# A cross-attention and mixture-of-experts kernel: first maximum behind the logits' copy, w2's first third behind w3, w2 and the turned h in two float32r parts

## What is computed

```python
# LayerNorm of x, then cross-attention with 16 heads of 16
Q = split_heads(layernorm(x) @ Wq + bq); K = split_heads(ctx @ Wk + bk); V = split_heads(ctx @ Wv + bv)
scores = einsum('bhqd,bhkd->bhqk', Q, K) / sqrt(16)
x = x + tanh(g_xattn) * (split_back(softmax(scores) @ V) @ Wo + bo)
# LayerNorm again, then a mixture of 8 experts, of which each row takes 2
xf = layernorm(x).reshape(-1, 256)
scores = softmax(xf @ w_router.T); expert_weights, expert_indices = top_k(scores, 2)
h = silu(einsum('td,edh->eth', xf, w1)) * einsum('td,edh->eth', xf, w3)      # 352 wide
y = einsum('eth,ehd->etd', h, w2)
x = x + tanh(g_ffn) * sum over the 2 chosen experts of expert_weight * y
```

## Time and profile before

| | |
|---|---|
| median of 3 runs | 848.33 us (844.21 to 849.57) |
| the profiled execution | 848.78 us, its span 847.0 us |
| mean granted TensorE clock | 0.989 of full speed |
| PE busy | 805.1 us (95%) |
| PEld busy | 696.9 us (82%) |
| POOL busy | 525.4 us (62%) |
| DVE busy | 490.0 us (58%) |
| ACT busy | 436.1 us (51%) |

### The profile page before, as it was taken

How to read it: one execution, slowest core, us unless ns; L and a number is a source line. 1 busy time by engine, 2 the same in 40 slices (tenths; PEclk the granted TensorE clock), 3 DMA queues, 4 the chain that set the end, 5 groups by cost and what they waited for, 6 DMA issues and landing times.

```text
span 847.0 us, 22216 instructions
## 1 busy us (share of the span) xinstructions
PE 805.1 (95%) x7529; PEld 696.9 (82%) x7529; DVE 490.0 (58%) x1170; ACT 436.1 (51%) x1120; POOL 525.4 (62%) x599
## 2 busy tenths in 40 slices
PE   7889999999999999999999999888999999999995
PEld 6679899998998999999999998756777777777773
DVE  5576777877877777787777777733622222222221
ACT  3356766766676676677666666554222222222221
POOL 6554555566576667657666765436677766666652
PEclk8899999999999999999999999999999999999998
DMA  6857867776676666676657565574344444443332
GB/s 159 209 142 175 200 171 191 191 191 169 168 183 162 153 160 154 160 183 149 149 135 172 135 162 136 149 195 78 52 63 64 73 66 64 63 63 64 63 58 30
DMA packets 99733, 112.33 MB, mean 133 GB/s; under 512 B 29164, under 2 KB 81012, under 8 KB 99624
## 3 DMA queue, kind: packets, MB, share of 16 engines
q1 hardware_dynamic: 79608, 92.48, 44.4%
q0 software_dynamic: 18512, 17.60, 13.4%
q10 hardware_dynamic: 1504, 0.85, 0.5%
HBM read 35.48 MB, written 17.53 MB: 63 GB/s over the span
## 4 chain that ended last, share of the span: by engine, by line
PE 70%; DVE 11%; SPq 8%; DMA 4%; issue 3%; POOL 1%; ACT 1%; ACTq 0%; POOLq 0%; DVEq 0%
PE ps L1473 17%; PE ps L1536 10%; PE ps L1212 8%; PE ps L1195 7%; PE ps L1226 6%; PE ps L1180 6%; DVE negmax L919 5%; PE ps L1219 3%; PE ps L1329 3%; PE ps L1388 2%; PE ps L1492 2%; SPq L285 2%; DMA w_sb<-in_L_ffn_w_dram 2%; SPq L286 2%; SPq L290 2%
## 5 line engine op out<-in xcount | busy, mean ns | idle before, releaser
L919 DVE TENSOR_REDUCE negmax<-ps 112x2 f32<-112x750 f32 x256 | 239.8, 938 | 111.1 <-PE ps L1212 102.9
L620 ACT ACTIVATE probs<-ps 125x448 f32<-125x448 f32 x384 | 208.9, 545 | 83.8 <-PE ps L1180 65.1
L399 POOL DMA_DIRECT2D stack<-negmax_t x128 | 68.3, 537 | 175.3 <-ACT negmax_t L675 164.2
L1180 PE MATMUL ps<-stack 97*125 97x224 f32 x768 | 163.7, 295 | 0.6 <-ACT probs L620 0.4
L1212 PE MATMUL ps<-stack 96*112 96x376 f32 x512 | 141.3, 357 | 14.2 <-DVE negmax L919 10.3
L523 POOL DMA_INDIRECT out_dram<-y,idx x63 | 100.8, 1600 | 69.4 <-issue 32.0
L1180 PEld LDWEIGHTS ps<-stack 97*125 97x125 f32 x768 | 126.2, 187 | 7.7 <-ACT probs L620 1.2
L719 ACT ACTIVATE silu<-ps 128x352 f32<-128x352 f32 x63 | 29.3, 465 | 188.2 <-PE ps L1473 161.9
L1131 DVE TENSOR_TENSOR h<-silu,ps 128x352 f32<-128x352 f32 x63 | 32.8, 520 | 143.9 <-PE ps L1473 138.9
L1536 PE MATMUL ps<-w_sb,h_t 128*128 x378 | 92.3, 380 | 3.1 <-DMA w_sb<-in_L_ffn_w_dram 2.4
L1212 PEld LDWEIGHTS ps<-stack 96*112 96x112 f32 x512 | 71.8, 178 | 23.7 <-DVE negmax L919 14.0
(11 more groups left out here) (239 smaller groups left out, 1500.5 us busy)
## 6 DMA issues: line engine op xcount, KB each, us to landing
stack<-split SPq DMA_DIRECT2D x252, 150.0 KB
stack<-split SPq DMA_DIRECT2D x127, 94.0 KB
ctx_raw<-in_ctx_dram SPq DMA_DIRECT2D x29, 375.0 KB, 3.9
stack<-split SPq DMA_DIRECT2D x127, 56.0 KB
out_dram<-xa SPq DMA_DIRECT2D x32, 112.0 KB, 2.4
xn_scratch<-xn SPq DMA_DIRECT2D x32, 112.0 KB
xa<-in_x_dram SPq DMA_DIRECT2D x7, 448.0 KB, 4.2
w_sb<-in_L_ffn_w_dram SPq DMA_DIRECT2D x16, 176.0 KB
```

Source lines behind the costliest of these rows:

```text
L399: gp.dma_start(dst[:, :, SKP + SQ * h:SKP + SQ * h + SQ], negmax_t[4 * h:4 * h + 4, half, :].bitcast(f32)).then_inc(s_nmrow[half][c % NSLO ...
L620: act.activation(probs[:, n % NP, :], ps[0:KW, EXPB + k % 2, 0:4 * SQ], ACT.Exp).then_inc(s_exp, 1)
L919: dve.tensor_reduce(negmax[:, half, :, p4], ps[0:SQ, m1:m2 + 1, 0:SK], axis=AX.X, op=ALU.max, negate=True).then_inc(s_max, 1)
L1180: last = pe.matmul(ps[0:KW, EXPB + k % 2, QW * m:QW * m + QW], stack[:, place_of(b), p, KW * ch:KW * ch + KW], stack[:, place_of(b), p, SK ...
```

## The change

1. **First maxima.** VectorE takes maximum 0 of the next batch at the end of slot 11 (from i = -1 on), behind the copy of `lg`; `bn_aggr`, `half2`, route part 3 and `xn` come behind it. Before it took it in slot 0 of the next iteration, behind `xn`. The copy of `lg` itself is moved ahead of `bn_aggr`.
2. **w2's first third** is loaded by SyncE right behind w3_hi, ahead of idx 0 to 3, instead of behind the stores.
3. **w2 and the turned h in two parts.** w2 is split into `w2_h` (rounded to float32r, by ScalarE) and `w2_l` (the rest, by VectorE), one expert in each of tiles 4 to 11 on ScalarE and 5 to 12 on VectorE (`SPLIT = 4`). From tile 13 on (`PARTS = 13`) ScalarE's copy of the turned h gives `ht_h`, VectorE subtracts it from the same PSUM bank to give `ht_l`, and the product is ht_h w2_h + ht_h w2_l + ht_l w2_h: nine float32r matmuls instead of three of fp32.
4. **The expert number** of tile t + 1 is loaded behind w1 of tile t, a tile ahead.
5. To make room, `ctx_l`, `ctx_h`, `ctx_raw` and `probs` of the attention loop move into the memory that the expert loop uses again.

```diff
-        ctx_l, ctx_h = sb("ctx_l", [P, NSLOT, DC, SKP], f32r), sb("ctx_h", [P, NSLOT, DC, SKP], f32r)
...
-        probs = sb("probs", [KW, NP, 4 * SQ])
...
-        ctx_raw = sb("ctx_raw", [P, DC, SK])
...
+        ctx_l, ctx_h = (late.enter_context(nc.sbuf_tensor(n, [P, NSLOT, DC, SKP], f32r)) for n in ("ctx_l", "ctx_h"))
+        ctx_raw = late.enter_context(nc.sbuf_tensor("ctx_raw", [P, DC, SK], f32))
+        probs = late.enter_context(nc.sbuf_tensor("probs", [KW, NP, 4 * SQ], f32))
...
+        ht_h, ht_l = (sb(n, [P, FC, P], f32r) for n in ("ht_h", "ht_l"))
+        w2_h, w2_l = (sb(n, [P, FC, NE, EMB], f32r) for n in ("w2_h", "w2_l"))
...
+        SPLIT, PARTS = 4, 13
...
+        def w2_parts(e):
+            n = F - P * (FC - 1)
+            return [tuple(w[:, 0:FC - 1, e, :] for w in (w2_sb, w2_h, w2_l)), tuple(w[0:n, FC - 1, e, :] for w in (w2_sb, w2_h, w2_l))]
...
                         sp.dma_start(w3_hi[:, e, :], w3[e, P:2 * P, :]).then_inc(s_w13, 16)
+                    sp.dma_start(w2_sb[:, 0, :, :], w2[:, 0:P, :].rearrange("e p d -> p e d")).then_inc(s_w2, 16)
                     for t in range(4):
                         load_idx(t)
                 if i == LAST - 1:
                     sp.wait_ge(s_nmrow[1][(B - 1) % NSLOT], 32 * ((B - 1) // NSLOT + 1))
-                    for c in range(FC):
+                    for c in range(1, FC):
                         n = min(P, F - P * c)
...
                     act.wait_ge(s_h_ps, t)
                     wait(act, s_y_ps, t - 1)
-                    act.activation(h_t[:, :, :], ps[:, HTB, 0:FC * P], ACT.Copy).then_inc(s_h_t, 1)
+                    if t - 1 < PARTS:
+                        act.activation(h_t[:, :, :], ps[:, HTB, 0:FC * P], ACT.Copy).then_inc(s_h_t, 1)
+                    else:
+                        act.activation(ht_h[:, :, :], ps[:, HTB, 0:FC * P].rearrange("p (c q) -> p c q", c=FC), ACT.Copy).then_inc(s_h_t, 1)
+                if 0 <= t - SPLIT < NE:
+                    if t == SPLIT:
+                        act.wait_ge(s_pv, 4 * B)
+                        act.wait_ge(s_w2, 16 * FC)
+                    for raw, high, low in w2_parts(t - SPLIT):
+                        act.activation(high, raw, ACT.Copy).then_inc(s_w2h, 1)
...
+            def maximum(c, t):
+                half, p4 = t // 4, t % 4
+                dve.wait_ge(s_max_ps, 8 * c + t + 1)
+                if p4 == 0:
+                    wait(dve, s_nm_ps, 2 * c + half - 1)
+                m1, m2 = max_banks(c, t)
+                dve.tensor_reduce(negmax[:, half, :, p4], ps[0:SQ, m1:m2 + 1, 0:SK], axis=AX.X, op=ALU.max, negate=True).then_inc(s_max, 1)
...
-                    if k in MAX_IN and c is not None:
-                        t = MAX_IN.index(k)
-                        half, p4 = t // 4, t % 4
-                        dve.wait_ge(s_max_ps, 8 * c + t + 1)
-                        if p4 == 0:
-                            wait(dve, s_nm_ps, 2 * c + half - 1)
-                        m1, m2 = max_banks(c, t)
-                        dve.tensor_reduce(negmax[:, half, :, p4], ps[0:SQ, m1:m2 + 1, 0:SK], axis=AX.X, op=ALU.max, negate=True).then_inc(s_max, 1)
+                    if k in MAX_IN and c is not None and (k > 0 or c == 0):
+                        maximum(c, MAX_IN.index(k))
                     if k == 10 and e is not None:
                         dve.wait_ge(s_x2, e + 1)
                         dve.bn_stats(st2[:, :], xrow(e)).then_inc(s_st2, 1)
...
+                    if k == 11 and i == GB * SNAP + 7:
+                        dve.wait_ge(s_tot, 1)
+                        link(dve.tensor_copy(n_rest[:, :], ps[0:1, BB_, CT:CT + NE]))
+                    if k == 11 and r is not None:
+                        dve.wait_ge(s_lg_ps, r + 1)
+                        dve.tensor_copy(lg[:, r // GB % 2, r % GB, :], ps[0:SQ, BB_, LG:LG + NE]).then_inc(s_lg, 1)
+                    if k == 11 and i >= -1 and live(i + 2) is not None:
+                        maximum(i + 2, 0)
                     if k == 11 and e is not None:
                         dve.wait_ge(s_st2, e + 1)
                         wait(dve, s_xn2, e - 1)
                         link(dve.bn_aggr(mv2[:, e % 2, :], st2[:, :]))
                         dve.tensor_scalar(half2[:, :], mv2[:, e % 2, 1:2], LN_EPS, -0.5, ALU.add, ALU.mult).then_inc(s_half2, 1)
-                    if k == 11 and i == GB * SNAP + 7:
-                        dve.wait_ge(s_tot, 1)
-                        link(dve.tensor_copy(n_rest[:, :], ps[0:1, BB_, CT:CT + NE]))
                     if (i, k) in MAP_AT:
                         early_map(MAP_AT.index((i, k)))
-                    if k == 11 and r is not None:
-                        dve.wait_ge(s_lg_ps, r + 1)
-                        dve.tensor_copy(lg[:, r // GB % 2, r % GB, :], ps[0:SQ, BB_, LG:LG + NE]).then_inc(s_lg, 1)
...
+                if t - 1 >= PARTS:
+                    dve.wait_ge(s_h_t, t)
+                    dve.tensor_tensor(ht_l[:, :, :], ps[:, HTB, 0:FC * P].rearrange("p (c q) -> p c q", c=FC), ht_h[:, :, :].bitcast(f32),
+                                      ALU.subtract).then_inc(s_htl, 1)
...
+                if 0 <= t - SPLIT - 1 < NE:
+                    for n, (raw, high, low) in enumerate(w2_parts(t - SPLIT - 1)):
+                        dve.wait_ge(s_w2h, 2 * (t - SPLIT - 1) + n + 1)
+                        dve.tensor_tensor(low, raw, high.bitcast(f32), ALU.subtract).then_inc(s_w2l, 1)
...
-            e_m = None
+            e_m, e_next = None, pe.value_load(e_idx[0:1, 0:1], min_val=0, max_val=NE - 1)
             for t in range(TILES + 1):
                 o, m, x1 = t - 1, t, t + 1
                 e_o = e_m
                 if m < TILES:
-                    e_m = pe.value_load(e_idx[0:1, m:m + 1], min_val=0, max_val=NE - 1)
+                    e_m = e_next
                     if m == 0:
                         pe.wait_ge(s_w13, 16 * DC * NE)
                     pe.wait_ge(s_xg_t, m + 1)
                     wait(pe, s_silu, m)
                     inner(m, (w1_sb[:, 0], w1_sb[:, 1]), AB, e_m, s_a)
+                    if x1 < TILES:
+                        e_next = pe.value_load(e_idx[0:1, x1:x1 + 1], min_val=0, max_val=NE - 1)
                 if o >= 0:
                     pe.wait_ge(s_h, o + 1)
                     wait(pe, s_h_t, o)
+                    wait(pe, s_htl, o - PARTS)
                     for c in range(FC):
                         last = pe.transpose(ps[:, HTB, P * c:P * c + P], h[:, P * c:P * c + P], ident[:, :])
                     last.then_inc(s_h_ps, 1)
...
                         pe.wait_ge(s_pv_t, B)
                     pe.wait_ge(s_h_t, o + 1)
                     wait(pe, s_y, o)
-                    for c in range(FC):
-                        n = min(P, F - P * c)
-                        last = pe.matmul(ps[:, YB, 0:EMB], h_t[0:n, c, :], w2_sb[0:n, c, bass.ds(e_o, 1), :].rearrange("p e d -> p (e d)"),
-                                         start=(c == 0), stop=(c == FC - 1))
+                    if o == PARTS:
+                        pe.wait_ge(s_w2l, 2 * NE)
+                    terms = ((h_t, w2_sb),) if o < PARTS else ((ht_h, w2_h), (ht_h, w2_l), (ht_l, w2_h))
+                    for j, (ht, w) in enumerate(terms):
+                        if j == 2:
+                            pe.wait_ge(s_htl, o - PARTS + 1)
+                        for c in range(FC):
+                            n = min(P, F - P * c)
+                            last = pe.matmul(ps[:, YB, 0:EMB], ht[0:n, c, :], w[0:n, c, bass.ds(e_o, 1), :].rearrange("p e d -> p (e d)"),
+                                             start=(j + c == 0), stop=(j == len(terms) - 1 and c == FC - 1))
                     last.then_inc(s_y_ps, 1)
```

1 line of the change is left out of this document (added).

## The result

The changed kernel takes 842.38 us (median of 14 runs, 840.14 to 846.46), the kernel before 847.89 us (median of 14). The ratio is 0.9941, with a 95% interval of 0.9918 to 0.9964: about 5 us, 0.6% faster, where 12.5 were forecast (848.33 to 835.8) and where 829.5 to 842.0 was the range. The profiled execution took 845.82 us.

What follows compares the result with a forecast made beforehand. TensorE was taken as the bound, busy 180.00 of 180 us in the expert loop. 848.78 - 2.5 (maxima) + 0.5 (w2's third) - 11.0 (product) + 0.5 (splitting) = 836.3, less 0.45 to the median: 835.8 us; range 829.5 to 842.

Steps and rivals of the forecast that it cites:

- w2's first third: Way into the expert loop: idx delayed 2.9 us, w2 wait of 2.4 saved; 0.5 us lost, bad end 3.6 lost.
- the wait for w2 of 2.41 us: At the first w2 product: TensorE's wait for the w2 weights, expected to vanish, 2.4 us gained.
- The maxima: Attention loop borders: 21 x 0.25 = 5.2 won, 6 x 0.44 = 2.7 lost behind routing; 2.5 us gained.
- A third term: Attention loop borders: half2 behind the maximum delays ScalarE's root and negmax_t by 0.5 us, costed at nothing.
- The product: Expert tiles 13 to 62: nine float32r matmuls of 0.12 make 1.08 instead of 1.30; 11.0 us gained.
- The splitting of w2: Tiles 4 to 12: copies and subtractions delay h of tile 9 by 0.4, table loads 0.1; 0.5 us lost.
- The expert number: Expert loop: its load of 0.30 us hides behind w1's passes, costing nothing; without that cover 15 us.
- D: Rival, way into the expert loop: idx isn't held up by w2's third; 832.9 us, chance 0.11.
- F: Rival: both small prices at their bad end, 3.6 lost at w2, nothing won by the maxima; 841.4 us, chance 0.09.

Runs made afterwards that it cites:

- b4: Changed kernel, first third of w2 still ahead of idx, the other two thirds held until the gather of tile 0 has landed; 839.82 us.
- d3: Changed kernel plus unread TensorE transposes: 14 ahead of the wait for the last batch's negmax rows, 76 ahead of the turn of tile 0; 843.65 us.
- a1: Changed kernel with w2's first third again loaded behind the stores, ahead of its other two thirds; 835.24 us, ratio to before 0.9863.
- a4: a1 with maximum 0 back in its old place behind xn, the copy of lg staying ahead of bn_aggr; 836.98 us.
- b3: a1 with the expert number again loaded ahead of w1 of its own tile; 838.85 us.
- c1: a1 with bn_aggr, half2, the copy of lg and r_slot all ahead of the moved maximum 0, only xn behind it; 832.86 us, ratio 0.9811.
- d1: Kernel before with one edit alone: first third of w2 loaded ahead of idx 0 to 3; 856.39 us, ratio 1.0122.
- d2: Kernel before with one part alone: maximum 0 moved ahead of xn, in the order of c1; 841.14 us, ratio 0.9938.

## Why the prediction was wrong

The forecast was 835.8 us, and 842.38 came. By its own steps:

- **w2's first third, the step that failed.** The forecast had "2.9 - 2.4 = 0.5 us lost", with 3.6 as its bad end. The way between the loops became 7.9 us longer, and putting the third back gave 7.1 us. Four things were wrong in that step. Its first term followed idx alone and took the lower price for it: from the issue of idx to the first gather it took 7.5 us instead of 3.6, 3.9 more, between the 2.9 and the 6.0 that the forecast had. It took the rest of the path as unmoved, but the late idx also carries the gather from ahead of the other 1792 KB to behind them: 7.1 us instead of 3.3, 3.8 more, which b4 gave back. It left the clock out: at its lower level the stretch from the turn of tile 0 to the first product takes 2 to 3 us more (d3, a1), though other kernels met this with idx on time. And what it set against these, the wait for w2 of 2.41 us, was in one profile only. Between the two profiles the parts add up: 0.2 (idx is issued later against the border) and 3.9 and 3.8 make the 8.0 up to the turn; behind it the slower clock took back about what the missing wait for w2 gave (15.13 against 15.21). On the other side stands what the forecast didn't see either: 1.5 us of the longer way hide the wait for `xn` of the last batch. Two of the sums in this step are slightly off: 1024 of 2816 KB at that pace are 6.1 us, not 6.0, and 1792 KB are 10.7, so w2 would be there by 568 and not 567. Neither moves the forecast.
- **The maxima.** 2.5 us were forecast; 2.0 came in the loop, or 1.5 by a4 against a1. Both are within the scatter of that column, so it isn't shown that the sum came near by more than luck; the terms can be compared by the single iterations. The terms were 0.25 won at an ordinary border (0.22 to 0.29 measured, with the part that the earlier copy of `lg` brings) and 0.44 lost behind routing (0.38 more than before). A third term was costed at nothing: "half2 delays ScalarE's root and with it negmax_t by 0.5 us". The delay was seen, its cover was looked for on ScalarE alone, and not on GpSimd, whose row DMA and `xn2` wait for that copy. The delay itself measured 0.33 (2.20 against 1.87). It costs 0.2 us against before, and 0.5 against what was to be had, in each of the four iterations in which the shifted `xn2` meets the cast.
- **The product.** 11.0 us forecast (50 x 0.22); 10.5 us in 49 steps, and 0.12 per matmul: mechanism and size right. No wait for `ht_l`, 0.8 us in hand, as worked out.
- **The splitting of w2.** 0.5 us forecast; in the profile of the changed kernel the products of the tiles 4 to 12 came 0.11 us later once (at tile 9). In the other kernels with this splitting it is 0.1 to 0.9 us in sum, most of it at the same tile, so the size was right as far as it can be seen.
- **The expert number** at nothing: right; without its cover b3 lost some 1.5 to 3.4 us, not 15.

With the third put back, the same terms give 848.33 - 2.5 - 11.0 + 0.5 = 835.3, and a1 measured 835.24. That it fits so closely is luck: in the profiles of a1 and before the tiles from 13 on gave 9.2 and the maxima 1.6, and the way was 2.1 shorter, without the wait for w2. Of the rivals none described what happened: D (idx not held up) was the opposite of it, F had both small prices at their bad ends and stopped at 841.4 because its bad end was 3.6.

## What to carry to other kernels

A large transfer put ahead of a small load on one queue costs more than the transfer's own time where the small load opens a chain of other DMAs: follow the chain to its last link, and see which bulk transfers that link now stands behind. A wait that one profile shows is no gain until a second execution shows it too, and a difference between two profiles is no result while kernels with the same code scatter as far. When a step is moved behind a longer one, follow what waits for it through every engine up to the next two meetings (here VectorE, ScalarE, GpSimd, and back to VectorE), and move only the one operation that has to move: c1 keeps everything but `xn` ahead of the maximum, and its loop is 4.4 us shorter than that of the changed kernel. Room behind a small transfer that others wait for seems to pay too: here the gather took 3.0 to 3.4 us with w2 issued 1.5 us or more behind it, and 3.8 to 5.6 with all of w2 issued closer.

## What the runs showed of the hardware

- A cast on VectorE (112x8, float32 to int32) takes 0.17 us with GpSimd silent. Where it meets the end of one GpSimd operation with a second right behind it, it takes 0.28 in some kernels (before, a4, c1, d1, d2) and 0.98 to 1.10 in the others; in the latter it ends 0.03 to 0.04 us behind the end of the second. The Trainium skill, page SBUF — State Buffer (Who interferes with whom), says that a cast can hold a pair of ports that VectorE shares with GpSimd, and that the later of the two is blocked until the other ends; the long casts agree, with one thing that the rule leaves open: the waiting cast can lose again to the next GpSimd operation. Not every cast waits: the one at 441.87 of the changed kernel takes 0.27 and ends 0.55 ahead of the end of the GpSimd operation that it lies inside. Why the cast won against the same pair of operations in the kernel before, in a4 and in c1 wasn't settled.
- 1024 KB in front of four loads of 1 KB made the first of them usable 7.5 us behind its issue instead of 3.6 (552.04 to 559.54; before 550.55 to 554.12), though the loads are tiny. The Trainium skill, page DMA: Bandwidth & Descriptors (Queues, rings and completion order), says that each DMA engine consumes one ring in order; the trace agrees. The gathers, which GpSimd issues on a queue of its own, are slowed too, to 7.1 and 9.0 us behind 1792 KB, and to 3.8 to 5.6 us where all of w2 is issued 0.4 to 1.0 us behind them, against 3.0 to 3.4 where it comes 1.5 us or more behind.
- A float32r matmul of 256 columns takes 0.12 us at the upper clock, both in the value projection and in this product.
- TensorE's clock fell to its lower level inside a wait of 2.0 us (553 to 556: 1.12 of 3 us busy, mean clock 0.89). It stayed there from 556 to 560 with 3.75 of 4 us busy, from 560 to 566 with 1.66 of 6 busy and from 566 to 572 with 5.34 of 6 busy, and was back at the upper level in the window from 572 to 578 (0.96).
- The first 60 us of the program vary by up to 4.7 us between the profiled executions (59.06 to 63.74 to the first values), with a granted clock of 0.83 to 0.96 between 20 and 60 us: 0.96 with the shortest, 0.84 with the longest.
